# Selective scan, windowed attention and routed FFN in fp32 on one core: the hand-off behind the last scan and the last tile's scatter rewritten

## What is computed

```python
x = x + selective_scan(einsum('bct,bcd->bdt', x, weights[conditions]), ...)   # 16 states for each feature
k, v, q = rms-normed and rotated projections of x; new keys and values go into a paged cache
a = softmax(q @ k_all.T * SCALE, window of 256 positions) @ v_all @ Wo        # 4 key heads, 8 query heads
idx = top_k(a @ w_r + b_r, half of the tokens of each sequence)
x = x + zeros.at[idx].set(gelu(a[idx] @ w1 + b1) @ w2 + b2)
```

## Time and profile before

| | before |
|---|---|
| median of three runs | 1847.52 us |
| the profiled execution's own time | 1847.98 us |
| its span, first to last instruction | 1846.2 us |
| TensorE busy | 1622.4 us (88%) |
| VectorE busy | 1442.8 us (78%) |
| ScalarE busy | 1280.3 us (69%) |
| GpSimd busy | 1253.8 us (68%) |
| mean granted TensorE clock | 0.97 |
| scan block ends | 925.5 us after the span's start |

### The profile page before, as it was taken

One profiled execution on the slowest core, in us unless ns is written; L12 is line 12 of the kernel. 1 busy time (PEld: TensorE's weight loads), 2 busy tenths in 40 slices (PEclk: granted clock), 3 DMA queues, 4 the chain that ended last, 5 costly groups with the idle time before them and its releaser, 6 DMA issues.

```text
span 1846.2 us, 30439 instructions
## 1 busy us (share of the span) xinstructions
PE 1622.4 (88%) x9591; PEld 1127.6 (61%) x9591; DVE 1442.8 (78%) x2552; ACT 1280.3 (69%) x4019; POOL 1253.8 (68%) x1134
## 2 busy tenths in 40 slices
PE   6788888888888888878777899999999999999996
PEld 5666565566666656555445665756667575665763
DVE  8999999999999999999867675656657565565521
ACT  6888888888888888876566664756557465665530
POOL 5789999999999999999767765445554444541000
PEclk9999999999999999998978999999999999999998
DMA  6435344334434434432366654334343333431010
GB/s 230 162 137 173 106 158 168 135 141 162 156 114 168 167 119 152 162 133 90 113 199 194 189 173 106 100 85 109 110 101 100 97 87 91 122 97 24 18 23 12
DMA packets 130007, 229.92 MB, mean 125 GB/s; under 512 B 31464, under 2 KB 82684, under 8 KB 124472
## 3 DMA queue, kind: packets, MB, share of 16 engines
q1 hardware_dynamic: 94456, 158.50, 25.1%
q0 software_dynamic: 35392, 69.48, 14.4%
HBM read 212.35 MB, written 43.65 MB: 139 GB/s over the span
## 4 chain that ended last, share of the span: by engine, by line
PE 41%; ACT 3%; issue 2%; POOL 2%; DVE 1%; DMA 1%; DVEq 0%; POOLq 0%; ACTq 0%
PE attn_psum L2001 12%; PE attn_psum L2017 12%; PE attn_psum L1949 4%; PE attn_psum L1936 4%; PE attn_psum L1929 4%; PE attn_psum L1920 2%; POOL kv_at L1554 1%; PE attn_psum L1910 1%; PE attn_psum L1961 1%; POOL kv_at L1546 1%; ACT xh L1675 1%; ACT th L1676 1%; DMA kv_at<-in_kv_rows,idx_old 1%; ACT prob L1638 0%; DMA kv_at<-kv_scratch,idx_new 0%
## 5 line engine op out<-in xcount | busy, mean ns | idle before, releaser
L1122 DVE TENSOR_TENSOR_SCAN hid<-scan_psum,hid 128x1024 f32<-128x1024 f32 x256 | 580.7, 2269 | 0.0
L1341 PE MATMUL scan_psum<-ident,hid 128*128 128x128 f32 x2048 | 342.4, 286 | 124.0 <-POOL hid L554 121.6
L1341 PEld LDWEIGHTS scan_psum<-ident,hid 128*128 128x128 f32 x2048 | 254.6, 146 | 282.7 <-POOL hid L554 156.1
L554 POOL TENSOR_TENSOR hid<-hid,kv_at 128x1024 f32<-128x1024 f32 x128 | 306.4, 2407 | 23.8 <-DVE hid L1122 23.4
L554 POOL TENSOR_TENSOR hid<-hid,bc 128x1024 f32<-128x1024 f32 x128 | 305.7, 2402 | 17.7 <-DVE hid L1122 17.0
L1782 DVE CUSTOM_DVE_ANT_0 prob<-attn_psum,mask 128x336 f32<-128x336 f32 x256 | 119.9, 504 | 235.9 <-PE attn_psum L1929 235.5
L1644 ACT COPY p_t<-attn_psum 112x384 f32<-112x384 f32 x256 | 122.3, 483 | 226.9 <-PE attn_psum L1936 226.9
L1546 POOL DMA_INDIRECT kv_at<-in_kv_rows,idx_old x183 | 177.5, 970 | 101.9 <-issue 51.2
L2017 PE MATMUL attn_psum<-w,ffn_hid 128*128 128x512 f32 x512 | 237.9, 595 | 5.0 <-DVE y_sb L1847 5.0
L1554 POOL DMA_INDIRECT kv_at<-kv_scratch,idx_new x189 | 196.4, 1039 | 65.8 <-issue 54.3
L2001 PE MATMUL attn_psum<-xs_in,w 128*128 128x256 f32 x1024 | 232.7, 381 | 7.7 <-ACT xs_in L1650 6.6
(11 more groups left out here) (225 smaller groups left out, 3016.4 us busy)
## 6 DMA issues: line engine op xcount, KB each, us to landing
bc<-bc_scratch SPq DMA_DIRECT2D x16, 2048.0 KB, 10.3
kv_at<-bc_scratch SPq DMA_DIRECT2D x15, 2048.0 KB, 9.9
q_scratch<-qg SPq DMA_DIRECT2D x32, 260.0 KB, 2.1
early<-q_scratch SPq DMA_DIRECT2D x32, 260.0 KB
x_pair<-in_x_pairs SPq DMA_DIRECT2D x32, 256.0 KB, 4.7
f_wo<-in_w_o SPq DMA_DIRECT2D x32, 256.0 KB, 3.3
out_t<-x_rows SPq DMA_DIRECT2D x64, 128.0 KB, 3.1
a_scratch<-a_sb SPq DMA_DIRECT2D x32, 256.0 KB, 2.6
```

The lines of the kernel that those rows point to most:

```text
L554: pool.tensor_tensor(hid[:, r, :, :], hid[:, r, :, :], bc[q // 2][:, 4 * j:4 * j + 4, 1, :], ALU.mult).then_inc(pool_hc, 1)
L1122: nc.vector.tensor_tensor_scan(states, decay[k % 2], states, 0.0, ALU.mult, ALU.add).then_inc(dve_h, 1)
L1341: mm = nc.tensor.matmul(yc[g], hid[:, e % RING, i, P * g:P * g + P], ident[:], start=False, stop=(k % 4 == 3 and i == 3), is_transpose=Tru ...
```

## The change

Keys of groups 30 and 31 become one entry: TensorE writes them to two neighbouring PSUM banks, ScalarE copies both at once, VectorE runs its operations over both groups (512 elements in place of 256), and the root is taken of both together. The rotation now reads the raw keys, and the scale is applied in the last operation. The two groups' queries share one sum over heads and one root. Eight of the matmuls of these entries change place: four of them go ahead of k = 6 of the last quarter, one ahead of k = 7, one ahead of the last `turn_x1`, and two behind it. The product's steps of the last quarter move from slots 20 to 23 to slots 8 to 11. ScalarE copies group 29's keys at k = 7 of the last quarter. SyncE stores the two groups' keys behind one wait, then the two groups' queries. Small tiles of these steps move from the state buffer `hid` to `sp_a`.

In the attention block, the last tile's rows of the output are gathered from DRAM into x_rows after these were transposed; VectorE adds b2 and later the FFN's result to them; a plain indirect DMA puts them back. The block's end leaves out the GpSimd drain.

```diff
@@ -104,7 +104,7 @@
         du = psum[:, 4, 0:2 * SUB].rearrange("p (c t) -> p c t", c=2)
         y = [psum[:, 5 + i, :] for i in range(2)]
         pro = psum[:, 7, :]
-        last_bank = [pro] + [psum[:, i, :] for i in range(4)]
+        last_bank = [psum[:, i, :] for i in range(4)]
 
...
-        LAST = [(NG - 3, 1), (NG - 2, 1), (NG - 1, 1), (NG - 2, 0), (NG - 1, 0)]
+        LAST_KEYS = [(NG - 3, 1), (NG - 2, 2)]
...
+                sp.wait_ge(act_lc, 3)
+                sp.wait_ge(dve_lk, 2)
+                for i in range(2):
+                    store_keys(NG - 2 + i, last_kv[:, i, :])
+                for i in range(2):
+                    g = NG - 2 + i
+                    sp.wait_ge(dve_lk, 3 + i)
+                    sp.dma_start(S["q"][g * GRP:g * GRP + GRP, :], qg[g % 2][:]).then_inc(st_q[g % 2], 16)
...
                     act.wait_ge(pe_fold, folds(n) + 1)
+                    if n == 4 * NT - 1:
+                        act.wait_ge(pe_turn, 2 * n + 1)
                     wait(act, st_w, 16 * n)
                     nc.scalar.copy(f_out[:], y[0][:, SUB:2 * SUB]).then_inc(act_fold, 1)
...
                         take_product(s - 1)
                         take_x1(t - 1, 3, 0)
-                        take_last(0)
-                        query_squares(s - 3, (q + 1) % 2, range(2, H))
+                        query_squares(s - 3, (q + 1) % 2, [2, 3])
                         last_rms(0)
+                        query_squares(s - 3, (q + 1) % 2, range(4, H))
                         sums(t - 1, 3, 1)
                         take_x1(t - 1, 3, 1)
                         key_rms()
-                        for n in range(1, len(LAST)):
-                            take_last(n)
-                            last_rms(n)
+                        take_last_keys()
+                        last_rms(1)
+                        take_last_queries(0)
+                        take_last_queries(1)
+                        last_rms(2)
...
+                    if k == 7 and s == 4 * NT - 1:
+                        take_third_last()
+
+
...
+            def take_last_keys():
+
+                act.wait_ge(pe_last, 1)
+                act.wait_ge(pe_fold, folds(4 * NT))
+                nc.scalar.copy(last_raw[1], psum[:, 0:2, 0:G * HD]).then_inc(act_lc, 1)
+                nc.scalar.copy(last_kv[:, :, G * HD:KV], psum[:, 0:2, G * HD:KV]).then_inc(act_lc, 1)
+
+            def take_last_queries(i):
+
+                p = (NG - 2 + i) % 2
+                act.wait_ge(pe_last, 2 + i)
+                act.wait_ge(st_q[p], 16 * (NG // 2 - 1))
+                nc.scalar.copy(qg[p][:, 0:D], last_bank[2 + i]).then_inc(act_lc, 1)
...
+                w = (G, 2 * G, 2 * H)[n]
...
+                dve.wait_ge(act_lc, n + 1)
+                link(v.tensor_tensor(sq_, raw, raw, ALU.mult))
+                v.reduce_sum(last_ss[n][:, 0:w], sq_.rearrange("p k (g d) -> p (k g) d", g=G), AX.X).then_inc(dve_ls, 1)
...
+                for i in range(k):
+                    for j in range(2):
+                        v.tensor_tensor(heads[1][:, i, :, HALF * j:HALF * j + HALF],
+                                        heads[0][:, i, :, HALF * (1 - j):HALF * (1 - j) + HALF],
+                                        last_sin[n][:, i, HALF * j:HALF * j + HALF].unsqueeze(1)
+                                        .to_broadcast([P, G, HALF]), ALU.mult)
...
+                link(v.tensor_tensor(total, total, turned, ALU.add))
+                r0, r3 = newton(n, w)
+                rs = last_rs[n][:, 0:w]
+                link(v.scalar_tensor_tensor(rs, r3, 1.5, r0, ALU.add, ALU.mult))
+                v.tensor_tensor(last_out(n)[:, :, 0:G * HD].rearrange("p k (g d) -> p k g d", g=G), heads[2],
+                                rs.rearrange("p (k g) -> p k g", k=k).unsqueeze(3).to_broadcast([P, k, G, HD]),
+                                ALU.mult).then_inc(dve_lk, 1)
...
+            def last_queries():
+
+                for i in range(2):
+                    raw = qg[(NG - 2 + i) % 2][:, 0:D]
+                    dve.wait_ge(act_lc, 4 + i)
+                    squares = v.tensor_tensor(q_sq[:, D * i:D * i + D], raw, raw, ALU.mult)
+                link(squares)
+                v.reduce_sum(last_ss[2], q_sq.rearrange("p (h d) -> p h d", h=2 * H), AX.X).then_inc(dve_ls, 1)
+                r0, r3 = newton(2, 2 * H)
+                for i in range(2):
+                    v.scalar_tensor_tensor(qg[(NG - 2 + i) % 2][:, D:QW], r3[:, H * i:H * i + H], 1.5,
+                                           r0[:, H * i:H * i + H], ALU.add, ALU.mult).then_inc(dve_lk, 1)
...
+                last_keys(0)
+                link(last_tables_of(1))
+                last_keys(1)
+                last_queries()
...
+                def last_keys(i, j):
+
+                    if j < 2 and i == j == 0:
+                        pe.wait_ge(act_x1, NCH * (2 * NT - 1) + 2)
                         pe.wait_ge(dve_h, 32 * NT - 1)
-                    nc.tensor.matmul(last_bank[1], x1[1][:, j, at:at + GRP], w_qkv[:, j, D * i:D * i + D],
-                                     start=(j == 0), stop=False)
...
+                    if j > 1 and i == 0:
+                        pe.wait_ge(act_x1, NCH * (2 * NT - 1) + j + 1)
+                    mm = nc.tensor.matmul(last_bank[i], x1[1][:, j, GRP * i:GRP * i + GRP], w_qkv[:, j, D:2 * D],
+                                          start=(j == 0), stop=(j == NCH - 1))
+                    if i and j == NCH - 1:
                         mm.then_inc(pe_last, 1)
+
+                def last_queries(i):
+
+                    if i == 0:
+                        pe.wait_ge(dve_h, 32 * NT)
+                    for j in range(NCH):
+                        mm = nc.tensor.matmul(last_bank[2 + i], x1[1][:, j, GRP * i:GRP * i + GRP], w_qkv[:, j, 0:D],
+                                              start=(j == 0), stop=(j == NCH - 1))
+                    mm.then_inc(pe_last, 1)
 
...
                 if isinstance(t, int) and t == NT and q == 0:
-                    last_start(0)
+                    last_keys(1, 2)
                     turn_x1(t - 1, 3, 1)
-                    last_start(1)
-                    last_start(2)
-                    last_groups()
+                    for i in range(2):
+                        last_keys(i, 3)
+                    for i in range(2):
+                        last_queries(i)
...
+                    if s == 4 * NT - 1 and k == 6:
+                        for j in range(2):
+                            for i in range(2):
+                                last_keys(i, j)
+                    if s == 4 * NT - 1 and k == 7:
+                        last_keys(0, 2)
...
-                        if parts.scan and 20 <= slot < 24:
-                            product(slot - 20)
+                        fold_at = 8 if s == 4 * NT - 1 else 20
+                        if parts.scan and fold_at <= slot < fold_at + NCH:
+                            product(slot - fold_at)
...
-        block = ctx.enter_context(nc.Block())
+        block = ctx.enter_context(nc.Block(no_gpsimd_drain=True))
...
+            def gather_sums(tt):
+
+                n = 2 * NTL - 2 + tt
+                pool.wait_ge(pe_xt, n + 1)
+                pool.indirect_dma_start(x_rows[tt][:], None, out,
+                                        bass.IndirectOffsetOnAxis(ap=r_idx[n % 4][:, 0:1], axis=0)
+                                        ).then_inc(ld_xg[tt], 16)
+
+            def put_rows(tt):
+
+                n = 2 * NTL - 2 + tt
+                pool.wait_ge(dve_y, n + 1)
+                pool.indirect_dma_start(out, bass.IndirectOffsetOnAxis(ap=r_idx[n % 4][:, 0:1], axis=0), x_rows[tt][:], None
+                                        ).then_inc(st_y, 16)
...
-            add_rows(NTL - 1, 0)
-            add_rows(NTL - 1, 1)
+            for tt in range(2):
+                gather_sums(tt)
+            for tt in range(2):
+                put_rows(tt)
             pool.wait_ge(st_y, 16 * 2 * NTL)
...
+            def add_sums(tt):
+
+                dve.wait_ge(ld_xg[tt], 16 * (NTL + 1))
+                v.tensor_tensor(x_rows[tt][:], x_rows[tt][:], b2[:], ALU.add).then_inc(dve_xs, 1)
+
+            def take_last_y(tt):
+
+                dve.wait_ge(dve_xs, tt + 1)
+                dve.wait_ge(pe_y, 2 * NTL - 1 + tt)
+                v.tensor_tensor(x_rows[tt][:], y_bank(NTL - 1, tt), x_rows[tt][:], ALU.add).then_inc(dve_y, 1)
+
...
-                        if w == 0:
+                        if w == 0 and j == 1 and last_tile(i - 2):
+                            add_sums(0)
+                            add_sums(1)
+                        if w == 0 and last_tile(i - 2):
+                            take_last_y(j - 1)
+                        elif w == 0:
                             take_y(i - 2, j - 1)
```

136 lines of the change are left out of this document (50 added, 86 removed).

## The result

The changed kernel takes 1836.52 us (median of 5, 1832.59 to 1838.56), the kernel before 1848.05 beside it (median of 5): ratio 0.9931, 95% interval 0.9916 to 0.9945, that is 12.8 us less by the ratio, between 10 and 15.5. Its profiled execution took 1836.52 us around a span of 1834.7, so 1.8 us lie outside, as before. The forecast was 1836.0 us. How well the forecast's parts hold is another question: the tail gave more than was reckoned for it, the hand-off perhaps less.

A forecast was written before the change was run, and what follows sets the result against it. TensorE had by far the largest share of the last-ending chain (41%), so gains were sought where the chain leaves it: 8.6 + 1.4 + 2.0 = 12.0 us off 1847.98 gives 1836.0 us, range 1832.5 to 1840.5 (8 in 10).

The forecast's parts named there:

- the tail: Kernel's end, behind the last bias add: 8.6 us gained by leaving out GpSimd's drain, 1.4 us by the last scatter.
- the hand-off: From scan block to attention block: an earlier barrier moves everything behind it, gain 2.0 us, bounds 0 to 3.0.
- The drain: End of the last block: GpSimd's DRAIN is not issued, its barrier semaphore follows at once, gain 8.6 us.
- put off: Rival at the kernel's end: what the drain waits for is waited for after the span; gain 3.4 us, chance 0.12.
- The last scatter: Last tile's output: a plain indirect write lands after 3.3 us, the accumulating one after 4.7; gain 1.4 us.
- The two gathers and two adds: Added for the last tile on GpSimd and VectorE: hidden in idle time, cost nothing; without that cover 3.4 us.
- TensorE at the hand-off: End of the scan block: projections move, sums of k = 7 end at 904.35, TensorE at 914.9 instead of 917.36.
- the rival with the low clock: At the hand-off: TensorE's clock level falls during 16.4 us of projection work, 4.4 us slower overall; chance 0.03.
- the third way: VectorE's first key operation meeting GpSimd's multiplications; forecast had two ways: it goes first, delaying GpSimd 0.4 us, or waits until 902.1.
- The barrier: Between scan and attention blocks: opens at 923.4 in place of 925.35, after query stores at 919.0 and 919.4.
- Everything shifted alike to the end: From the barrier to the kernel's end: all work moves earlier by the same amount, the hand-off's 2.0 us.
- my own test: Attention and FFN, barrier to last bias add (906.1 us): growing by more than 1 us would show the forecast wrong.

The follow-up runs named there:

- e1: Kernel before with one line changed, the attention block ending without the GpSimd drain: 1841.04 us, ratio 0.9957.
- e6: Changed kernel with the last quarter's four product steps back in their old place (k = 5): 1836.13 us, ratio 0.9936 to the kernel before.
- e4: Changed kernel with SyncE's stores of the last keys issued before the second half of its early loads, first time: 1834.03 us, ratio 0.9922 to the kernel before.
- e8: Same kernel as e4 (last keys' stores ahead of the second half of the early loads), second time: 1834.75 us, ratio 0.9936 to the kernel before.
- e12: Same kernel as e4 (last keys' stores ahead of the second half of the early loads), third time: 1837.93 us, ratio 0.9944 to the kernel before.
- e3: Changed kernel with the old accumulating scatter and the last block's drain put back, leaving only the hand-off's change: 1847.33 us, ratio 0.9988 to the kernel before.
- e10: Kernel before with both changes of the tail (no drain, last tile's sums gathered and put back plainly), old hand-off: 1838.13 us, ratio 0.9948.
- e7: The changed kernel run again, unaltered, for a second profile: 1837.76 us, ratio 0.9946 to the kernel before.
- e11: The changed kernel run again, unaltered, for comparison on the same chip: ratio 0.994 to the kernel before.
- e5: Kernel before with a GpSimd drain added at the end of the scan block too: 1850.12 us, ratio 1.0009.

## Why the prediction was right, and where not

**The drain** (reckoned 8.6): right. 8.6 us less between GpSimd's wait and its semaphore, 7.9 by e1's times; 1.8 us outside the span, so the rival "put off" is out.

**The last scatter** (1.4, bounds -0.2 to 1.6): the mechanism was right, the size not. The put lands 2.7 us after its issue, not 3.3, and the gain is 2.0, beyond the upper bound of 1.6. The row that I took as nearest, a gather of the same 128 rows, is no measure for a write of them. The estimate from the Trainium skill, page "DMA: Bandwidth & Descriptors", section "Anatomy of one DMA — SWDGE (gpsimd) path", was 2.6 us and a gain of 2.1: the trace agrees with that page within 0.1 us, and I had put the row above it.

**The two gathers and two adds** (nothing): right. The gathers stand ahead of 38.68 us of GpSimd's idle time; the adds lie before VectorE's 8.92.

**TensorE at the hand-off:** right step by step. Sums of k = 7 over at 904.1 (904.35), last query projection at 914.6 (914.9), granted clock 1.00 from 898.3 to 914.6, so the rival with the low clock did not come there. e6 confirms that the product's move is worth 1.0 us on TensorE.

**VectorE:** it met GpSimd, but in the third way, which I had not written down: the first key operation went first (899.00, 0.61 us), and the small table operation behind it took 1.92 us where its twin takes 0.24, beside GpSimd's multiplication. It was hidden. Keys were over at 913.4 (913.9).

**The barrier** (923.4, came at 921.96): forecast 1.4 us too late. Of the 3.4 us gained (2.0 reckoned), 0.45 are the earlier end of the scan in this execution. The stores left at 918.7 and 919.05 (919.0, 919.4), and GpSimd's semaphore came 2.9 us behind the second, where I had 3.66 and 0.3 for sharing.

**What follows the barrier:** here the step failed. I had let GpSimd's three first gathers "start near 918.1, end near 922, before the barrier". They wait for the keys' stores. Of these I had priced SyncE's queue (914.2, came 914.6), and given 3.4 us from the second store (914.7) to the first gather, about what the last key store of before needed (issued 916.2, gather 919.3). It took 5.3: 4.3 until the landing of the store issued at 915.05, and 1.0 from there to the gather at 920.30. The barrier fell open in front of a GpSimd that was not ready, and of the barrier's 2.9 us (behind the scan's end) 1.7 reached the attention block. e4, e8 and e12 show that it is these stores that GpSimd's first gather hangs on, and that SyncE's queue costs it some 1.2 us; why their landing is slow was not isolated.

**"Everything shifted alike to the end":** wrong for the stretch from the barrier to GpSimd's first gather, which takes 1.2 us back; behind that it holds in the mean, but not from one execution to the next. What reached GpSimd's first gather (1.7 us in the first profiles, 1.9 in the mean) is about what reached the end (1.9 ± 1.3 at the last add; in times e3 1.6 ± 0.7, e10 1.4 ± 1.1). In single executions TensorE's waits for gathers near 994 and 1020 and the lower clock level behind them move all that follows by up to some 5 us. So my own test, the span from the barrier to the last add, says little from one profile: it grew by 2.6 us (908.7 for 906.1), beyond the 1 us that I had set, but in e7 it is 904.3 and in e11 906.0, and over the four old and four new profiles it grew by 1.0 us, no more than their scatter.

So 1836.0 came out because 8.6 + 2.0 + 1.5 is 12.1, and I had 8.6 + 1.4 + 2.0. The scatter's miss of 0.6 us is measured; the hand-off's of 0.5 is inside its error. Within the hand-off two misses cancel, and that is luck: the barrier came 0.9 us earlier than reckoned, behind the scan's end, and the keys' stores took 1.2 us of it away again.

## What to carry to other kernels

Look behind the last landing: what an engine does between its last wait and the end of the span stands in no list of busy time, and here it was two thirds of the gain. When a barrier is brought forward, follow each engine to its first instruction that needs data, and price the landing behind what is queued ahead of it; here the path from the keys' stores to GpSimd's gathers took over. And a gain in the middle of a kernel has to pass every wait and every change of clock behind it, which here moved single executions by more than the gain, so measure it at landmarks down to the end, over several executions, before it is counted.

## What the runs showed of the hardware

- GpSimd's drain takes 8.6 to 8.8 us at the kernel's end, behind the last landing. At the scan block's end it lasts 6.9 us (e5), 4.1 of them behind GpSimd's last issue. What its length goes by is open.
- A plain indirect write of 128 rows of 2 KB lands 2.7 us after issue, the accumulating one 4.6 to 5.2, the gather in most cases 3.3. Their issue takes 0.98, 1.55 and 0.99 us.
- The key stores of 256 KB issued right behind queued loads landed after 2.9 to 4.7 us, in different executions of one program after 3.5 and after 4.4. The query stores of 260 KB, issued some microseconds later, landed after 2.0 to 2.5 us, and where GpSimd's gathers had begun before them (before and e6, for instance) the last one took 3.1 to 3.8.
- A VectorE operation of 0.24 us took 1.92 beside a GpSimd multiplication, though the VectorE operation just before had not been held.
- TensorE's lower level comes for some 3 or some 7 us in one execution and not in the next. Near 1023 that costs about 1 or 2 us; together with the waits for a gather ahead of it, it makes the 4.4 us between two executions of one kernel.
